# Per-tile normalisation of the projection and a reordered entry of the recurrence in a four-layer conditioned residual stack

## The reference, cut to what matters

```python
xr, gate = jnp.split(x @ W_in.T, 2, axis=-1)
xr = xr + t_emb[:, None, :]
xc = silu(causal_conv4(xr) + b_conv)
mu, var = xc.mean(-1), xc.var(-1)
xn = (xc - mu) / jnp.sqrt(var + 1e-05) * ln_g + ln_b
Bm, Cm, dt = jnp.split(xn @ W_xproj.T, 3, axis=-1)
dt = jnp.tanh(dt @ W_dt.T + b_dt) * 0.01
Ad = 1.0 + dt * -jnp.tanh(A_log)
Bd = Bm * jnp.minimum(jnp.linalg.norm(xn, axis=-1, keepdims=True), 1.0)
# per step: h = clip(h * ad + bd x xt, -10, 10); yt = ct . h
y = ys + D * xn
return y * silu(gate) @ W_out.T
```

## Time and profile before

| what | us |
|---|---|
| median of 3 runs | 4079.85 |
| lowest and highest | 4077.65 and 4083.68 |
| the profiled execution, its own time | 4080.76 |
| its span in the trace | 4078.5 |

### The profile page before, as it was taken

How to read it: one execution, slowest core, us unless ns; L and a number is a source line. 1 busy time by engine, 2 the same in 40 slices (tenths; PEclk the granted TensorE clock), 3 DMA queues, 4 the chain that set the end, 5 groups by cost and what they waited for, 6 DMA issues and landing times. The chain is left out here.

```text
span 4078.5 us, 63717 instructions
## 1 busy us (share of the span) xinstructions
PE 3758.9 (92%) x22112; PEld 2311.1 (57%) x22112; DVE 3019.3 (74%) x3172; ACT 1333.6 (33%) x2013; POOL 1875.4 (46%) x1444
## 2 busy tenths in 40 slices
PE   8999669999997899999879999997999839999999
PEld 6777423333443677777656777765777613433334
DVE  4776679999996677776457777753666768999997
ACT  3555411111112444344244444433555501111111
POOL 2655635555553134444313444432455635555554
PEclk9999859999998899999979999998999959999999
DMA  3666745656564112222222222223466665656563
GB/s 119 242 239 244 291 167 168 193 177 189 180 187 142 56 62 85 79 79 67 79 95 62 84 79 80 71 73 126 184 248 248 264 211 161 196 174 193 176 189 122
DMA packets 270514, 619.95 MB, mean 152 GB/s; under 512 B 34112, under 2 KB 36928, under 8 KB 270304
## 3 DMA queue, kind: packets, MB, share of 16 engines
q1 hardware_dynamic: 265952, 608.74, 44.7%
q10 hardware_dynamic: 4352, 8.39, 0.6%
HBM read 380.58 MB, written 236.45 MB: 151 GB/s over the span
## 5 line engine op out<-in xcount | busy, mean ns | idle before, releaser
L1156 DVE CUSTOM_DVE_ANT_0 l0r_g<-l0r_g,l0r_pv,l0r_cf 128x1024 f32<-128x1024 f32 x512 | 674.4, 1339 | 70.9 <-PE l0r_pv L962 48.7
L1156 DVE CUSTOM_DVE_ANT_0 l3r_g<-l3r_g,l3r_pv,l3r_cf 128x1024 f32<-128x1024 f32 x512 | 673.9, 1339 | 71.2 <-PE l3r_pv L962 49.4
L974 PE MATMUL l0r_py<-l0r_g,l0r_cd 128*32 128x512 f32 x2048 | 283.0, 627 | 0.1
L962 PE MATMUL l3r_pv<-l3r_x,l3r_wv 32*128 32x512 f32 x1024 | 261.6, 510 | 22.8 <-POOL l3r_wv L882 16.6
L974 PE MATMUL l3r_py<-l3r_g,l3r_cd 128*32 128x512 f32 x2048 | 281.8, 624 | 0.1
L962 PEld LDWEIGHTS l3r_pv<-l3r_x,l3r_wv 32*128 32x128 f32 x1024 | 97.3, 187 | 325.3 <-issue 205.2
L962 PE MATMUL l0r_pv<-l0r_x,l0r_wv 32*128 32x512 f32 x1024 | 262.2, 511 | 21.1 <-POOL l0r_wv L882 15.8
L962 PEld LDWEIGHTS l0r_pv<-l0r_x,l0r_wv 32*128 32x128 f32 x1024 | 97.6, 188 | 324.6 <-issue 205.6
L591 DVE SCALAR_TENSOR_TENSOR l0a_pacc<-l0a_pad,l0a_wconv,l0a_pacc 128x512 f32<-128x512 f32 x192 | 144.8, 754 | 35.5 <-ACT l0a_pacc L456 31.0
L591 DVE SCALAR_TENSOR_TENSOR l3a_pacc<-l3a_pad,l3a_wconv,l3a_pacc 128x512 f32<-128x512 f32 x192 | 144.8, 754 | 34.1 <-ACT l3a_pacc L456 29.5
L102 PE MATMUL l2h_ps_p<-l2h_xh,l2c_wh 128*128 128x512 f32 x384 | 161.3, 420 | 2.5 <-DVE l2h_xl L1830 2.1
(11 more groups left out here) (455 smaller groups left out, 9892.1 us busy)
## 6 DMA issues: line engine op xcount, KB each, us to landing
l0r_x<-xhl_s SPq DMA_DIRECT2D x128, 512.0 KB, 11.5
l3r_x<-xhl_s SPq DMA_DIRECT2D x128, 512.0 KB, 11.5
xhl_s<-l0a_xo SPq DMA_DIRECT2D x116, 512.0 KB, 4.6
xhl_s<-l3a_xo SPq DMA_DIRECT2D x116, 512.0 KB, 4.6
gate_s<-l0a_gate SPq DMA_DIRECT2D x64, 256.0 KB, 2.9
l0r_dx<-dx_s SPq DMA_DIRECT2D x32, 512.0 KB, 13.2
l0r_gate<-gate_s SPq DMA_DIRECT2D x32, 512.0 KB, 13.8
l0r_crow<-feed_s SPq DMA_DIRECT2D x64, 256.0 KB
```

The source lines that it names most:

```text
L962: last = pe.matmul(pv[j % 2][:, h * HALF:(h + 1) * HALF], wv[r, q, 2 * t + j % 2, :], x[r, q, t, j % 2, :], start=True, stop=True)
L974: last = pe.matmul(py[j * JW:(j + 1) * JW, h * HALF:(h + 1) * HALF], cd[:, q, t, j, :], g[:, t, j, h * HALF:(h + 1) * HALF], start=t == 0, ...
L1156: dve._custom_dve(bass.dve_ops.TENSOR_ADD_SAT, out=g[:, t, j, :], in0=g[:, (t - 1) % TS, j, :], in1=pv[j % 2][:, :], s0=cf[:, q, t, 0, j:j ...
```

## The change

It has three parts, in both scan layers.

1. The four correcting operations are done per tile in the projection phase on 128 x 192 (`fit_projection`): for tiles 0 to 5 after the taps of column group 2 two tiles later, for tiles 6 and 7 at the end of DVE's stream. The square root is done on POOL there as well, on 128 x 4 per tile (`size`).
2. In the entry, the low half of the feed is made ahead of one of the two bound computations, and SP issues the x rows of block 1 and the `dx` and `gate` rows of block 0 behind the feed's stores and loads.
3. DVE, not POOL, multiplies the feed rows of block 0 by the mask.

```diff
+            def fit_projection(T):
+                rows = slice(T * TB, (T + 1) * TB)
+                shape = [P, TB, NPROJ]
+                for step in range(4):
+                    if step == 0:
+                        dve.wait_ge(proj_ev, T + 1)
+                        dve.wait_ge(rstd, TB * (T + 1))
+                        last = dve.tensor_tensor(mean_w[:, :, :], stat[:, rows, 0].unsqueeze(2).to_broadcast(shape),
+                                                 wsum[:, :].unsqueeze(1).to_broadcast(shape), ALU.mult)
...
+                    last.then_inc(fitted, 1)
+                    dve.wait_ge(fitted, 4 * T + step + 1)
...
                     add_taps(T, it)
+                    if it == 2 and T >= 2:
+                        fit_projection(T - 2)
...
             keep_projection(NT - 1)
+            for T in (NT - 2, NT - 1):
+                fit_projection(T)
...
+            def size(T):
+                pool.wait_ge(ss, TB * (T + 1))
+                pool.tensor_tensor(stat[:, T * TB:(T + 1) * TB, 3], stat[:, T * TB:(T + 1) * TB, 3], half[:, :].to_broadcast([P, TB]),
+                                   ALU.pow).then_inc(sized, 1)
...
                     if first and q == 0:
                         load_x(0, 0)
-                        load_x(1, 1)
-                        load_tokens(0, 0)
                         store_feed()
                         load_feed(0, 0)
                         load_feed(1, 1)
+                        load_x(1, 1)
+                        load_tokens(0, 0)
...
                         bounds(0, 0)
-                        weigh(0, 0, 1)
+                        pool.wait_ge(wvm, 1)
...
             pe.wait_ge(const, 48)
-            pe.wait_ge(step, 8)
+            pe.wait_ge(step, 4)
...
-            chain(dve.tensor_tensor(mean_w, stat[:, :, 0].unsqueeze(2).to_broadcast(full),
-                                    wsum[:, :].unsqueeze(1).to_broadcast(full), ALU.mult))
-            chain(dve.tensor_tensor(proj[:, :, :], proj[:, :, :], mean_w, ALU.subtract))
-            chain(dve.tensor_tensor(proj[:, :, :], proj[:, :, :], stat[:, :, 2].unsqueeze(2).to_broadcast(full), ALU.mult))
-            chain(dve.tensor_tensor(proj[:, :, :], proj[:, :, :], wbias[:, :].unsqueeze(1).to_broadcast(full), ALU.add))
...
-            chain(dve.tensor_scalar(out[0], inv, CLIP, None, ALU.mult))
             dve.wait_ge(feed_high, 1)
             dve.tensor_tensor(feed_l.rearrange("s j i -> s (j i)"), pf, feed_h.bitcast(F32).rearrange("s j i -> s (j i)"),
                               ALU.subtract).then_inc(feed_low, 1)
+            chain(dve.tensor_scalar(out[0], inv, CLIP, None, ALU.mult))
             chain(dve.tensor_scalar(out[1], inv, -CLIP, None, ALU.mult))
             dve.memset(g[:, TS - 1, :, :], 0.0).then_inc(gup, GJ)
+            dve.wait_ge(const, 48)
+            dve.wait_ge(cr_ld[0], 32)
+            dve.tensor_tensor(wv[:, 0, :, :], crow[:, 0, :, :], same[:, :].unsqueeze(1).to_broadcast([P, 2 * TS, P]), ALU.mult)\
+               .then_inc(wvm, 1)
```

More of the change, by code:

```diff
@@ L150, in project_phase @@
         dx = ph.sb("dx", [P, DI])
+        mean_w = ph.sb("mean_w", [P, TB, NPROJ])
+        half = ph.sb("half", [P, 1])
         junk = ph.sb("junk", [P, DI], mybir.dt.bfloat16)
@@ L166, in project_phase @@
             "loaded", "folded", "copied", "scaled", "summed", "kept"))
+        fitted, sized = ph.sem("fitted"), ph.sem("sized")
         zeroed, halved, paired = ph.sem("zeroed"), ph.sem("halved"), ph.sem("paired")
@@ L623, in keep_projection @@
                                 pp[:, 0:TB * NPROJ].rearrange("p (b c) -> p b c", b=TB)).then_inc(proj_ev, 1)
+            def fit_projection(T):
[7 more added lines that the diff above has]
+                                                 wsum[:, :].unsqueeze(1).to_broadcast(shape), ALU.mult)
+                    elif step == 1:
+                        last = dve.tensor_tensor(proj[:, rows, :], proj[:, rows, :], mean_w[:, :, :], ALU.subtract)
+                    elif step == 2:
+                        last = dve.tensor_tensor(proj[:, rows, :], proj[:, rows, :], stat[:, rows, 2].unsqueeze(2).to_broadcast(shape),
+                                                 ALU.mult)
+                    else:
+                        last = dve.tensor_tensor(proj[:, rows, :], proj[:, rows, :], wbias[:, :].unsqueeze(1).to_broadcast(shape),
+                                                 ALU.add)
+                    last.then_inc(fitted, 1)
+                    dve.wait_ge(fitted, 4 * T + step + 1)
             def fold_gain():
@@ L641, in _ @@
             dve.memset(mhalf[:, :], -0.5).then_inc(halved, 1)
+            dve.memset(half[:, :], 0.5).then_inc(halved, 1)
             dve.memset(ones[:, :], 1.0).then_inc(scaled, 1)
@@ L679, in _ @@
                 add_taps(NT - 1, it)
+                if it == 2:
+                    fit_projection(NT - 3)
             for b in range(TB):
@@ L717, in low_half @@
                 pool.tensor_tensor(split_rows(n)[:, 1, :], xn[:, r, :], split_rows(n)[:, 0, :].bitcast(F32), ALU.subtract).then_inc(xol, 1)
[L719 removed]
+            pool.wait_ge(halved, 2)
             for c in range(NW):
                 low_weight(c)
+            def size(T):
+                pool.wait_ge(ss, TB * (T + 1))
+                pool.tensor_tensor(stat[:, T * TB:(T + 1) * TB, 3], stat[:, T * TB:(T + 1) * TB, 3], half[:, :].to_broadcast([P, TB]),
+                                   ALU.pow).then_inc(sized, 1)
             pool.wait_ge(folded, 1)
@@ L734, in _ @@
                     skip_term(n)
+                if n % TB == 1 and n > TB:
+                    size(n // TB - 1)
+            size(NT - 1)
 def recurrence_phase(nc, tag, x_in, x_out, w, cst, dram, proj, stat, wsum, wbias, coef):
@@ L765, in recurrence_phase @@
         acol = ph.sb("acol", [P, 2])
-        half = ph.sb("half", [P, 1])
         norm = ph.sb("norm", [P, B])
-        mean_w = g[:, 0, 0:2, :].rearrange("p a d -> p (a d)")[:, 0:B * NPROJ].rearrange("p (b c) -> p b c", b=B)
         parts = [g[:, 0, 2, 0:512], g[:, 0, 2, 512:1024], g[:, 0, 3, 0:512]]
@@ L774, in recurrence_phase @@
         pf = pv[1][:, 512:1024]
-        alog_ld, root, step, turned, tanh = (ph.sem(n) for n in ("alog_ld", "root", "step", "turned", "tanh"))
+        alog_ld, step, turned, tanh = (ph.sem(n) for n in ("alog_ld", "step", "turned", "tanh"))
         fed, feed_turned, feed_high, feed_low, stored = (ph.sem(n) for n in (
@@ L872, in _ @@
         def _(pool):
-            pool.memset(half[:, :], 0.5).then_inc(root, 1)
-            pool.wait_ge(root, 1)
-            pool.tensor_tensor(norm[:, :], stat[:, :, 3], half[:, :].to_broadcast([P, B]), ALU.pow).then_inc(root, 1)
             pool.wait_ge(const, 48)
-            pool.wait_ge(step, 8 + 3 + GJ + 1 + 3)
+            pool.wait_ge(step, 4 + 3 + GJ + 1 + 3)
             def weigh(k, q, uses):
@@ L1110, in chain @@
                 dve.wait_ge(step, count[0])
-            full = [P, B, NPROJ]
-            chain(dve.tensor_tensor(mean_w, stat[:, :, 0].unsqueeze(2).to_broadcast(full),
-                                    wsum[:, :].unsqueeze(1).to_broadcast(full), ALU.mult))
-            chain(dve.tensor_tensor(proj[:, :, :], proj[:, :, :], mean_w, ALU.subtract))
-            chain(dve.tensor_tensor(proj[:, :, :], proj[:, :, :], stat[:, :, 2].unsqueeze(2).to_broadcast(full), ALU.mult))
-            chain(dve.tensor_tensor(proj[:, :, :], proj[:, :, :], wbias[:, :].unsqueeze(1).to_broadcast(full), ALU.add))
             part = [c.rearrange("p (b n) -> p b n", b=B) for c in parts]
@@ L1120, in _ @@
             chain(dve.tensor_copy(part[1], proj[:, :, NS:2 * NS]))
-            dve.wait_ge(root, 2)
-            chain(dve.tensor_scalar(norm[:, :], norm[:, :], 1.0, None, ALU.min))
+            chain(dve.tensor_scalar(norm[:, :], stat[:, :, 3], 1.0, None, ALU.min))
             chain(dve.tensor_tensor(part[0], proj[:, :, 0:NS], norm[:, :].unsqueeze(2).to_broadcast([P, B, NS]), ALU.mult))
```

1 line of the change is left out of this document (removed).

## The result

The changed kernel takes 4092.52 us (median of 6 runs, 4087.4 to 4097.25); the kernel before took 4077.57 beside it (6 runs). The ratio is 1.0035, with a 95% interval of 1.0023 to 1.0048. Measured once more later it took 4090.86 against 4078.9, ratio 1.0031 (1.0020 to 1.0041). So the change makes the kernel 12 to 15 us **slower**, where 4083 within 4073 to 4089 was forecast. The profiled execution took 4092.34 us, with a span of 4090.5; before it was 4080.76 and 4078.5.

The account below looks back on a forecast made before the run. The prediction took the blocks to run at DVE's pace, helped along by PE, leaving only once-per-layer work to win. Entries cost 1.2 us and the projection 2.0, so +3.2 on 4079.85: 4083 us, range 4073 to 4089.

Parts of the forecast that it names:

- Part 4: Projection phase: five fits cost 0, the sixth, in the last tile, 1.0 us; loss 1.0 us per layer, 2.0 in all.
- The line through free durations: DVE operation times from 1.76 us for 1536 elements and 0.69 for 512, giving 0.36 for 192 columns.
- The middle tiles, the fits at the end, `size`: Projection phase: five fits, fits seven and eight and POOL's square root all run in idle or waiting time, cost 0.
- Rival D: Projection's middle tiles: the fits are on the path, 15 us more, 4098; chance 0.03.
- Part 1: Head of the entry: four DVE operations leave, gain 2.5 us of 7.2; the other 4.7 become a wait for `ymask`.
- Part 2: Order in the entry: block 0's feed rows land 10.9 us after issue; loss 1.1 us in L0, 0.3 in L3.
- Part 3: Weighing of block 0 in the entry: 1.23 us on DVE instead of 2.34 on POOL, gain 1.1 us.
- What is late next: After the first spread: late output weights make PE wait 3 us for block 0's gating; the two entries cost 1.2 us.
- Rival A: Entries keep their gain, as the weights come less than some 6 us late: -3.8 us, 4076; chance 0.25.
- Rival B: PE's wait for the gating is longer, weights from 12.6 us late; at 14 us late, 4091; chance 0.12.
- Rival C: PE's clock rises before block 1, up to 6 us gained per layer, 4066; chance 0.10 for over 8 us.
- The count of the weights: Entry: first output weights arrive 27.8 us after the first feed load's issue, 10.1 us later in L0, 9.3 in L3.

Follow-up runs that it names:

- old loads: Changed kernel with block 1's x rows, `dx` and `gate` issued ahead of the feed's stores again: 4079.97 us, ratio 1.0007 to the kernel before.
- block 2's rows early: Changed kernel with tile 5's fit at the projection's end and block 2's feed rows loaded behind the first two output weights: 4073.89 us, ratio 0.9988.
- the run with the fit at the end: Changed kernel with tile 5's fit moved from the last tile to the end of the projection: 4080.28 us, ratio 1.0010 to the kernel before.
- the repeat: The changed kernel measured once more with no edit: 4090.86 us, ratio 1.0031 to the kernel before.
- the run with fit at the end and old loads: Changed kernel with tile 5's fit at the projection's end and block 1's x rows, `dx` and `gate` ahead of the feed's stores: 4073.64 us, ratio 0.9989.

## Why the prediction was wrong

- **Part 4, the last tile. This is the step that failed.** I priced the sixth fit at four operations of 0.36 us, "between 0 and 1.5 us on the path", and took 1.0. It costs 5.5 and 5.9 by the stretches, 5.7 by the four operations themselves. The line through free durations holds where POOL pauses, or where an input lies in PSUM; I never looked at what POOL does where the fit goes. A row of the trace of before, which I had not put beside this term, had the price: L569 at 232.44 took 2.11 us instead of 0.69 (shown above). The discount for the DMA drain was wrong too: from the last evacuation to the entry it takes 59.9 us before and 60.2 after, so nothing is absorbed. The range was too narrow for the same reason. With 5.7 in place of 1.0 per layer the sum is 4079.85 + 1.2 + 11.4 = 4092.5. That it meets the measured 4092.52 so closely is luck: in the profiled execution the two entries with the stretch behind them gave 1.5 us back where the sum has a loss of 1.2, and the rows that I put down to the clock made up for it.
- **The middle tiles, the fits at the end, `size`**: right, 0. From tile 1 to the end of tile 6 in L0 the two traces run in step (1.6 to 1.5 us apart). Rival D falls.
- **Part 1**: right in kind, and in size for L0: 2.75 us gained of 7.2, the rest a wait for `ymask`, which released PE 6.4 us after DVE's first operation (6.6 forecast). In L3 it was 7.7, and only 1.5 us were gained; the forecast had taken L3 to be like L0.
- **Part 2**: wrong, and small. The feed rows of block 0 took 9.9 us in L0, 0.1 more than before, and 9.7 in L3, 0.9 less, where 10.9 was forecast for both. No run shows a cost of the x rows behind them clear of the scatter.
- **Part 3**: right, 1.23 us and 1.1 gained. The first spreads came 3.7 and 3.4 us earlier relative to the entry (2.5 and 3.3 forecast). In L3 the forecast was met by luck: 1.0 less at the head and 1.2 more at the feed rows.
- **What is late next**: the mechanism was right, shown by taking it away in two ways (old loads; block 2's rows early). The first weight came 26.4 and 27.6 us after the feed's issue (27.8). PE's wait, 3 us in the forecast, was 0.7 in L0 and 5.6 + 1.2 in L3, 3.4 and 6.3 in the run with the fit at the end, 5.2 and 4.9 in the repeat: 4.5 on average, and 4 over all six kernels with the new order and block 2's rows late (the 1.2 is a wait for the read-out masks `cd`, which POOL makes just before). Its spread has two sources. One is PE's clock: where PE runs faster in the blocks before, it wants the gating earlier. In the changed kernel's L3 the granted clock was 0.79 to 1.00 from 15 to 33 us after the first spread, and PE came to its transposes 42.7 us after it; in its L0 it stayed at 0.50 for 60, and PE came after 46.1. The other is the gating itself, which was done 46.3 to 50.2 us after the first spread. Against the kernel before, from the entry's first operation, the transposes came 2.2 us earlier in L0 and 0.7 later in L3 in the profiled execution, and 0.8 later and 0.1 earlier in the repeat (0.5 and 0.7 later forecast).
- **Rival A** falls as I put it, since PE did wait, if only 0.7 us in the profiled L0. **Rival B** named the right side and the wrong place: it wanted the weights 12.6 us late, and relative to the entry's first operation they were 8.5 us later in L0 and 10.2 in L3 (10.1 and 9.3 forecast). **Rival C**: the clock rose early in some entries and not in others, with the same code (in L0's blocks 25 us after the first spread in the repeat, and not for 60 in the first profile), so it is scatter of a few us, not an effect of the moved entry. Its sum was also 2 us off: 4076 less twice 6 is 4064, not 4066.
- **The count of the weights** calls the slowest dimension of the feed's source a broadcast of 4. It is four rows, each broadcast to 16 partitions; the number that the count uses, four DMA engines, is the same.

## What to carry to other kernels

When an operation is moved on VectorE, look up in the timeline what GpSimd does at that very place. In these runs an operation that reads from SBUF alone lasted as long as the GpSimd operation beside it, and a chain of short ones paid once for each of GpSimd's. Move it by one step into a GpSimd pause, or give it an input in PSUM. And when loads are postponed for the sake of an earlier transfer, follow the queue to the next load that stands behind them: here two loads of 256 KB behind eight weights held up PE, through POOL's order, at a step that needs no weights.

## What was new about the hardware

- A DVE operation of 0.36 us took 2.43 beside a POOL operation of 2.38, and the next in the chain lost again to POOL's next one, which started 0.07 us after its predecessor and so before DVE's. Copies from PSUM at the same place took 0.357 us each. Not every POOL operation does it: beside the small power `size` (128 x 4, recorded as 1.13 us) they took 0.36.
- The effect acts the other way too: beside DVE's rescaling at the end of the phase, one of POOL's operations took 3.38 us (in the kernel before at 471.38, in the run with fit at the end and old loads at 471.61) instead of 2.4.
- Small stores are not small behind large loads: with 5 MB issued ahead of them and the DMA engines at a share of 1.03, two stores of 256 KB landed after 6.3 and 6.9 us instead of 2.2.
